# Opening of a four-layer graph network on one core: zero-padded node vectors, another order of fetches and sums

## The reference

```python
# block 0, _L0_gnn_ref (both supports are adj)
def _conv(x, adj):
    return x * jnp.sum(adj, axis=1)[None, :, None]
adaptive = jax.nn.softmax(jax.nn.relu(node_vec1 @ node_vec2), axis=1)   # 512x10 @ 10x512
outputs = [x]
for adj in (support0, support1, adaptive):
    x1 = _conv(x, adj)
    outputs.append(x1)
    for _ in range(2, ORDER + 1):
        x1 = _conv(x1, adj)
        outputs.append(x1)
out = jnp.concatenate(outputs, axis=2) @ W + b

# block 1, _L1_gnn_ref
A_norm = A + jnp.eye(n)
deg = jnp.sum(A_norm, axis=0) + jnp.sum(A_norm, axis=1) - jnp.diagonal(A_norm)
dinv = jax.lax.rsqrt(deg)
A_hat = A_norm * dinv[:, None] * dinv[None, :]
agg = jnp.einsum('nm,bmd->bnd', A_hat, features)
# then two linear layers with batch norms, relu between them
```

## Time and profile before

| | |
|---|---|
| Median of 3 runs | 937.22 us (935.61 to 937.93) |
| Profiled execution | 935.11 us |
| Its span in the profile | 933.3 us |
| TensorE (PE) busy | 893.1 us, 96% |
| VectorE (DVE) busy | 671.3 us, 72% |
| ScalarE (ACT) busy | 564.8 us, 61% |
| GpSimd (POOL) busy | 327.6 us, 35% |
| Instructions | 14540 |

### The profile page before, as it was taken

One profiled execution on the slowest core, in us unless ns is written; L12 is line 12 of the kernel. 1 busy time (PEld: TensorE's weight loads), 2 busy tenths in 40 slices (PEclk: granted clock), 3 DMA queues, 4 the chain that ended last, 5 costly groups with the idle time before them and its releaser, 6 DMA issues.

```text
span 933.3 us, 14540 instructions
## 1 busy us (share of the span) xinstructions
PE 893.1 (96%) x4990; PEld 774.3 (83%) x4990; DVE 671.3 (72%) x1589; ACT 564.8 (61%) x1230; POOL 327.6 (35%) x531
## 2 busy tenths in 40 slices
PE   9899999988989899999999999999999999999996
PEld 6788886366777689989989898998889898978986
DVE  6789996776687676677676767767776777675744
ACT  6477675944655565477457647765774775476341
POOL 3856554820122511362144216303521531340121
PEclk9999999999999899999999999999999999999999
DMA  5321201320110101001101200120110001001000
GB/s 186 136 68 62 74 36 46 135 87 6 34 58 1 34 1 57 2 23 35 57 1 46 69 1 12 35 69 1 46 39 31 12 12 46 1 12 34 1 23 24
DMA packets 26595, 38.55 MB, mean 41 GB/s; under 512 B 3333, under 2 KB 12422, under 8 KB 26010
## 3 DMA queue, kind: packets, MB, share of 16 engines
q1 hardware_dynamic: 26088, 36.05, 11.5%
q10 hardware_dynamic: 434, 1.57, 0.5%
HBM read 21.89 MB, written 15.73 MB: 40 GB/s over the span
## 4 chain that ended last, share of the span: by engine, by line
PE 50%; DVE 10%; ACT 8%; POOL 7%; issue 3%; ACTq 0%; DVEq 0%; POOLq 0%
PE psum L141 14%; PE psum L143 14%; PE psum L142 14%; PE psum L1867 2%; PE psum L1863 2%; PE psum L1864 2%; ACT gate L1438 2%; POOL out_rstd L1371 1%; ACT raw L1469 1%; POOL node_l L1389 1%; POOL x_rstd L1371 1%; ACT x L1469 1%; ACT raw L1532 1%; DVE cell L1584 1%; ACT gate L1441 1%
## 5 line engine op out<-in xcount | busy, mean ns | idle before, releaser
L1438 ACT ACTIVATE gate<-psum,gate_bias 128x256 f32<-128x256 f32 (+2 forms) x296 | 143.8, 557 | 67.7 <-PE psum L1867 54.4
L141 PE MATMUL psum<-in_h,wih_h 128*128 128x256 f32 (+2 forms) x312 | 106.8, 342 | 8.7 <-DVE in_l L1605 5.0
L143 PE MATMUL psum<-in_h,wih_l 128*128 128x256 f32 (+2 forms) x312 | 103.5, 332 | 0.0
L142 PE MATMUL psum<-in_l,wih_h 128*128 128x256 f32 (+2 forms) x312 | 103.1, 330 | 0.0
L141 PEld LDWEIGHTS psum<-in_h,wih_h 128*128 128x128 f32 x312 | 59.0, 189 | 21.2 <-DVE in_l L1605 8.6
L1405 POOL TENSOR_TENSOR gate<-in_h,in_l 128x512 f32<-128x512 f32 x14 | 17.9, 1306 | 157.5 <-DVE in_l L1605 157.5
L1441 ACT ACTIVATE gate<-cell 128x512 f32<-128x512 f32 (+2 forms) x80 | 40.3, 503 | 49.5 <-DVE cell L1589 39.1
L1586 DVE TENSOR_TENSOR gate<-gate 128x256 f32<-128x256 f32 (+2 forms) x48 | 24.1, 502 | 58.8 <-ACT gate L1438 58.7
L141 PE MATMUL psum<-e_h,shared 128*128 128x384 f32 x180 | 62.0, 344 | 2.2 <-POOL e_l L1420 2.0
L142 PEld LDWEIGHTS psum<-in_l,wih_h 128*128 128x128 f32 x312 | 59.2, 190 | 5.1 <-issue 0.2
L143 PEld LDWEIGHTS psum<-in_h,wih_l 128*128 128x128 f32 x312 | 58.9, 189 | 4.7
(11 more groups left out here) (394 smaller groups left out, 2894.2 us busy)
## 6 DMA issues: line engine op xcount, KB each, us to landing
x_spill<-x SPq DMA_DIRECT2D x30, 256.0 KB, 2.0
xt<-in_x_t_dram SPq DMA_DIRECT2D x16, 256.0 KB, 2.6
raw<-x_spill SPq DMA_DIRECT2D x16, 256.0 KB, 2.8
o_spill<-xt SPq DMA_DIRECT2D x14, 256.0 KB, 2.0
xt<-o_spill SPq DMA_DIRECT2D x14, 256.0 KB, 3.4
x<-x_spill SPq DMA_DIRECT2D x14, 256.0 KB, 3.6
out_dram<-raw SPq DMA_DIRECT2D x14, 256.0 KB, 2.3
raw<-in_adj_t_dram ACTq DMA_DIRECT2D x1, 1024.0 KB, 8.8
```

The costliest lines, as they stand in the source:

```text
L141: pe.matmul(dst, lh, rh, start=start, stop=False, **kw)
L142: pe.matmul(dst, lh, rl, start=False, stop=False, **kw)
L143: return pe.matmul(dst, ll, rh, start=False, stop=stop, **kw)
L1438: nc.scalar.activation(gate[q][:, 0:n], banks[GATE_BANK[q]][:, 0:n], ACT.Tanh if q == 2 else ACT.Sigmoid, bias=gate_bias[:, p - 1, q:q + 1 ...
```

## The change

- `nv1s` and `nv2s` become all 128 partitions of their regions. VectorE fills both with zeros behind `ones`; SP waits for that (`cleared`, 2) before it issues anything. The vectors still land in the first 10 partitions, and the logits matmuls contract over 128.
- Eight matmuls on `ones` instead of four.
- The transposed adjacency is issued on SP's queue, behind `adjn`, instead of on ScalarE's.
- The sums of three row tiles on VectorE come before the maximum of logits tile 3. ScalarE copies the bias rows before exp of tile 1. Exp of tile 3 goes between the scales of tiles 0 and 1, the last row tile's sum behind scale of tile 1, followed by all four column sums.
- Scale of tile 0 waits for the three row sums alone, that of tile 3 for the last one.
- In slot 0, combine of tiles 0 and 1 is cut in two: blocks 2 and 0 of both tiles, then the softmax factors, then blocks 3 and 4 of both, then the last row's copy and square, then `ask_dinv`. Tiles 2 and 3, and all later slots, are combined whole, with block 0 last as before.

```diff
@@ -178,7 +178,7 @@
         mix = sb("mix", [P, 2, 2, NT, D])
         aggh, aggl = sb("aggh", [P, 2, N], F32R), sb("aggl", [P, 2, N], F32R)
         z = sb("z", [P, HT, B, N])
-        nv1s, nv2s = z[0:RANK, 0, 0, :], z[0:RANK, 0, 1, :]
+        nv1s, nv2s = z[:, 0, 0, :], z[:, 0, 1, :]
         diag, squares = (z[:, 1, i, :].rearrange("p (t d) -> p t d", d=P) for i in range(2))
         spread_out = z[:, 0, 8:13, :].rearrange("p b n -> p (b n)")
         ahat = spread_out[:, 0:NT * N].rearrange("p (t n) -> p t n", n=N)
@@ -264,11 +264,13 @@
 
         @block.sync
         def _(sp):
-            sp.dma_start(nv1s, nv1_t).then_inc(c_nv, 16)
-            sp.dma_start(nv2s, nv2).then_inc(c_nv, 16)
+            sp.wait_ge(cleared, 2)
+            sp.dma_start(nv1s[0:RANK, :], nv1_t).then_inc(c_nv, 16)
+            sp.dma_start(nv2s[0:RANK, :], nv2).then_inc(c_nv, 16)
             for i in range(2):
                 sp.dma_start(xt[:, i, :], x_t[i]).then_inc(xt_loaded[i], 16)
             sp.dma_start(adjn[:], adj_n).then_inc(c_adjn, 16)
+            sp.dma_start(adjt, adj_t).then_inc(c_adjt, 16)
             for dst, src in ((w1raw, w1_t), (w2[:], w2_t), (bn1s[:], bn1), (bn2s[:], bn2), (wgs[:], wg), (bihs[:], bih), (bhhs[:], bhh)):
                 sp.dma_start(dst, src).then_inc(c_rest, 16)
 
@@ -436,7 +438,6 @@
             act.dma_start(ident[:], eye).then_inc(c_w, 16)
             act.dma_start(wraw[:], l0_w).then_inc(c_w, 16)
             act.dma_start(bias0[:], l0_b).then_inc(c_w, 16)
-            act.dma_start(adjt, adj_t).then_inc(c_adjt, 16)
 
             def split_x(q, i):
                 act.wait_ge(xt_loaded[i], 16 * (q + 1))
@@ -469,20 +470,23 @@
             relu_logits(1)
             relu_logits(2)
             exp_logits(0)
-            exp_logits(1)
             relu_logits(3)
-            exp_logits(2)
-            act.wait_ge(c_adjn, 16)
-            nc.scalar.activation(adjn[:, NT - 1, :], adjn[:, NT - 1, :], ACT.Identity, accum_out=coef[:, 0, NT - 1:NT]).then_inc(row_summed, 1)
-            exp_logits(3)
-            act.wait_ge(bias_spread, 1)
+            act.wait_ge(pe_setup, NT + 1)
             for i in range(2):
                 ins = nc.scalar.copy(bias_rows[:, i, :], tile(banks[3][:], 0))
             ins.then_inc(bias_ready, 1)
+            exp_logits(1)
+            exp_logits(2)
+
+            def sum_last_row():
+                act.wait_ge(c_adjn, 16)
+                nc.scalar.activation(adjn[:, NT - 1, :], adjn[:, NT - 1, :], ACT.Identity, accum_out=coef[:, 0, NT - 1:NT]).then_inc(row_summed, 1)
 
             def scale_first(q, t):
                 act.wait_ge(prod_done, NT * q + t + 1)
                 if q == 0 and t == 0:
+                    act.wait_ge(rows_summed, 1)
+                if q == 0 and t == NT - 1:
                     act.wait_ge(row_summed, 2)
                 nc.scalar.activation(mix[:, q % 2, :, t, :], scaled_block(t, 1), ACT.Identity,
                                      scale=coef[:, 0, t:t + 1]).then_inc(scaled, 1)
@@ -540,13 +544,14 @@
                 if now:
                     scale_first(q, 0)
                 if q == 0:
-                    sum_columns((0, 1))
+                    exp_logits(3)
                 if one and q > 1:
                     norm(q - 1, 0, range(NT))
                 if now:
                     scale_first(q, 1)
                 if q == 0:
-                    sum_columns((2, 3))
+                    sum_last_row()
+                    sum_columns(range(NT))
                 if q == 1:
                     norm(0, 0, range(NT))
                     split_ahat()
@@ -622,7 +627,8 @@
         def _(dve):
             chain = Chain(dve, dve1)
             roots = Roots(asked, rooted, exponent)
-            nc.vector.memset(ones[:], 1.0).then_inc(ones_ready, 1)
+            nc.vector.memset(ones[:], 1.0).then_inc(cleared, 1)
+            nc.vector.memset(z[:, 0, 0:2, :], 0.0).then_inc(cleared, 1)
 
             dve.wait_ge(c_w, 48)
             nc.vector.tensor_tensor(wmix[:, 0, :], wraw[:, 0, :], ident[:], ALU.add)
@@ -639,16 +645,22 @@
             nc.vector.tensor_tensor(wmix_l[:], wmix, f32(wmix_h[:]), ALU.subtract).then_inc(weights_ready, 1)
             logits_max(1)
             logits_max(2)
+            dve.wait_ge(c_adjn, 16)
+            nc.vector.reduce_sum(coef[:, 0, 0:NT - 1], adjn[:, 0:NT - 1, :], AX_X).then_inc(rows_summed, 1)
             logits_max(3)
-            dve.wait_ge(c_adjn, 16)
-            chain.link(nc.vector.reduce_sum(coef[:, 0, 0:NT - 1], adjn[:, 0:NT - 1, :], AX_X))
-            dve.wait_ge(row_summed, 1)
-            nc.vector.tensor_copy(row_sums[:], coef[:, 0, :]).then_inc(row_summed, 1)
-            nc.vector.tensor_tensor(coef[:, 1, :], coef[:, 0, :], coef[:, 0, :], ALU.mult)
-            dve.wait_ge(exp_ready, NT)
-            chain.link(nc.vector.reciprocal(smax[:, 3, :], smax[:, 2, :]))
-            chain.link(nc.vector.tensor_tensor(coef[:, 2, :], smax[:, 2, :], smax[:, 3, :], ALU.mult))
-            chain.link(nc.vector.tensor_tensor(coef[:, 3, :], coef[:, 2, :], coef[:, 2, :], ALU.mult))
+            dve.wait_ge(rows_summed, 1)
+            chain.link(nc.vector.tensor_tensor(coef[:, 1, 0:NT - 1], coef[:, 0, 0:NT - 1], coef[:, 0, 0:NT - 1], ALU.mult))
+
+            def softmax_sums():
+                dve.wait_ge(exp_ready, NT)
+                chain.link(nc.vector.reciprocal(smax[:, 3, :], smax[:, 2, :]))
+                chain.link(nc.vector.tensor_tensor(coef[:, 2, :], smax[:, 2, :], smax[:, 3, :], ALU.mult))
+                chain.link(nc.vector.tensor_tensor(coef[:, 3, :], coef[:, 2, :], coef[:, 2, :], ALU.mult))
+
+            def last_row():
+                dve.wait_ge(row_summed, 1)
+                nc.vector.tensor_copy(row_sums[:], coef[:, 0, :]).then_inc(row_summed, 1)
+                chain.link(nc.vector.tensor_tensor(coef[:, 1, NT - 1:NT], coef[:, 0, NT - 1:NT], coef[:, 0, NT - 1:NT], ALU.mult))
 
             def ask_dinv():
 
@@ -662,7 +674,7 @@
             def scale_ahat():
 
                 dve.wait_ge(dinv_spread, 1)
-                dve.wait_ge(pe_setup, NT + 1)
+                dve.wait_ge(pe_setup, NT + 2)
                 for t in range(NT):
                     ins = nc.vector.scalar_tensor_tensor(out=ahat[:, t, :], in0=adjt[:, t, :], scalar=dinv[:, t:t + 1],
                                                          in1=banks[7][:], op0=ALU.mult, op1=ALU.mult)
@@ -674,14 +686,20 @@
                 dve.wait_ge(dinv_squared, 1)
                 nc.vector.tensor_tensor(on_diagonal, on_diagonal, squares, ALU.add).then_inc(ahat_ready, 1)
 
-            def combine(q, t):
+            def combine(q, t, blocks=(2, 3, 4, 0)):
 
                 m = mix[:, q % 2, :, t, :]
                 dve.wait_ge(scaled, NT * q + t + 1)
-                for k in (2, 3, 4):
-                    chain.link(nc.vector.scalar_tensor_tensor(out=m, in0=scaled_block(t, k), scalar=coef[:, k - 1, t:t + 1],
-                                                              in1=m, op0=ALU.mult, op1=ALU.add))
-                nc.vector.tensor_tensor(m, m, scaled_block(t, 0), ALU.add).then_inc(mixed, 1)
+                for k in blocks:
+                    if k == 0:
+                        ins = nc.vector.tensor_tensor(m, m, scaled_block(t, 0), ALU.add)
+                    else:
+                        ins = nc.vector.scalar_tensor_tensor(out=m, in0=scaled_block(t, k), scalar=coef[:, k - 1, t:t + 1],
+                                                             in1=m, op0=ALU.mult, op1=ALU.add)
+                    if k == blocks[-1] and blocks != (2, 0):
+                        ins.then_inc(mixed, 1)
+                    else:
+                        chain.link(ins)
 
             def count_z(q, i):
                 b = 2 * q + i
@@ -733,11 +751,17 @@
                 nc.vector.tensor_tensor(low, whole, f32(high), ALU.subtract).then_inc(kept_lo, 1)
 
             def slot(q, now, more, one, two):
-                if now:
+                if q == 0:
+                    for t in range(2):
+                        combine(q, t, (2, 0))
+                    softmax_sums()
+                    for t in range(2):
+                        combine(q, t, (3, 4))
+                    last_row()
+                    ask_dinv()
+                elif now:
                     combine(q, 0)
                     combine(q, 1)
-                if q == 0:
-                    ask_dinv()
                 if q == PAIRED:
                     norm_last()
                     for i in range(2):
@@ -825,14 +849,14 @@
                 for _ in range(times):
                     pe.matmul(banks[bank][:], wmix_h[:, 0, :], operand[:, 0:N], start=True, stop=True)
 
-            pe.wait_ge(ones_ready, 1)
-            for _ in range(4):
+            pe.wait_ge(cleared, 1)
+            for _ in range(8):
                 pe.matmul(tile(banks[0][:], 0), ones[:], ones[:], start=True, stop=True)
```

(4 more changed lines are left out.)

4 lines of the change are left out of this document (2 added, 2 removed).

## The result

The changed kernel takes 938.99 us (median of 14 runs, 937.52 to 940.66) against 935.86 for the kernel before (14 runs, 935.01 to 938.6): a ratio of 1.0031, 95% interval 1.0023 to 1.0040, or 2.9 us slower. The range held it, by 2 us at its upper end; the case that the prediction thought likeliest, +0.7 us and no measurable difference, is not what happened. The ratio is just past the 0.3% that was given 0.12, and its interval lies on both sides of it.

A forecast was written before the change was run, and what follows sets the result against it. TensorE is busy 96% of the span, but VectorE carries the opening; 1.2 us gained before the first combine, 0.8, 0.6, 0.3 and 0.2 spent behind it, net +0.7: 937.22 becomes 937.9. Range 935.4 to 940.7, each widened by 0.3 noise.

The forecast's parts named there:

- the case that the prediction thought likeliest: Opening: gains given back in the split mix, without a fall of the clock; +0.7 us, 937.9 us, 45%.
- the 0.3% that was given 0.12: Whole kernel: chance 0.12 of being slower by over 0.3% (2.8 us).
- Zero fill and its wait on SP: Before the logits: fill 0.9 us, node vectors land at 4.5; warming matmuls start logits at 4.9, 1.7 us later.
- Zero rows: 128-row logits matmuls: zeros cost nothing; clock rises somewhere in the first two, if 128 rows count for it.
- S: Time in us of the first relu, on tile 0's logits: taken as 6.7, spanning 6.1 to 7.0.
- Three engines up to the first combine: VectorE, ScalarE, TensorE in the opening arrive within 0.3 us; first combine at 13.8 instead of 14.98, 1.2 us gained.
- The halved mix: Slot 0, tiles 0 and 1: 0.8 us waiting for tile 1, 0.6 softmax, 0.3 last row, 0.2 links spent.
- The stop behind it: TensorE idles 3.25 us before tile 2's products; a clock fall would cost tile 2 up to 0.6 us, tile 3 1.2.
- Adjacency: Copy by rows lands about 9.8 instead of 11.4 us; the transposed one near 12.7, its delay costing nothing.
- The case with this mechanism: Rival: TensorE's stop before tile 2 drops the clock; +0.7 plus 0.6 to 1.5 us, 939.0 as the middle, 22%.

The follow-up runs named there:

- with ten rows: The changed kernel with 10-row logits, no zero fill, no SP wait and four warming matmuls: 940.38 us, 1.0049 against the kernel before.
- the staged halves: The staged kernel with the mix of tiles 0 and 1 in halves again, nothing else: 938.19 us, 1.0016 against the kernel before.
- `W` behind: The changed kernel with the fetch of `W` on ScalarE's queue held back until the node vectors have landed: 946.68 us, 1.0100 against the kernel before.
- the filled stop: The changed kernel with 14 unused matmuls into a free bank in TensorE's slot 0 stop behind tile 1's products: 937.73 us, 1.0019 against the kernel before.
- the two runs with the zero rows: The kernel before with zero fill, SP's wait, 128-row logits, eight warming matmuls: 940.75 us; the same with the transposed adjacency behind the other on SP's queue: 936.43 us.
- the run with the zero rows alone: The kernel before with only the zero fill, SP's wait, 128-row logits and eight warming matmuls: 940.75 us, 1.0048.
- the staged kernel: The changed kernel, node vectors fetched aside and copied over cleared rows, no SP wait, mix whole, exp of tile 3 early, six warming matmuls, four later: 935.25 us.
- the order alone: The changed kernel with 10-row logits, no fill or SP wait, four warming matmuls, mix whole, exp of tile 3 before the first scale: 936.43 us, 0.9996.
- the mix whole again: The changed kernel with tiles 0 and 1 combined whole, after the softmax factors: 937.63 us, 1.0015 against the kernel before.

## Why the prediction was partly right

The range held, the likeliest case did not, and that 937.9 lies within 1.1 us of the measured 938.99 is luck: it was counted from 937.22, the median of three runs, where 14 give 935.86. The change itself was forecast at +0.7 us and measured at 2.9 to 3.1. At combine of tile 2 the forecast had +0.7 and the trace has +3.3. The 2.6 us between them are 1.5 at the first combine (15.32 instead of 13.8), 1.4 waiting for tile 2's products where none was forecast, and -0.3 in the halves. By its own steps:

- **Zero fill and its wait on SP**: the fill of 0.9 us was right (0.91). The landing at 4.5 was wrong: it reused the 2.0 us from issue to landing of the earlier trace rows for a transfer that the same wait had moved behind `W`. It landed at 5.83 in the changed kernel, at 8.0 with the transposed adjacency ahead too, and by 4.24 with neither. This is the step that failed first. The text looked at what SP's wait delays, and not at what overtakes it on the other queue.
- **Zero rows**: that they cost nothing was right (at the low level a record starts every 0.85 us with 128 rows, 7.70 to 8.56, as with ten), and that the clock rises in them too; the moment was not. The forecast had it in the first two logits matmuls (S = 6.7); in the changed kernel the clock rose in the third and S was 7.94. In other executions the eight records took 3.70 us from the first one on (5.61), so this term has a spread of a microsecond and more. By the rule of the Trainium skill (TensorE: Matmul & The Clock Gate, Part 1: The HAM clock gate), that the level follows how busy the engine has recently been, ten rows and 128 should have behaved alike. The trace disagrees: ten-row logits stayed at loads of 330 ns for 7.19 us, and those of 128 rows reached 190 ns at 10.18.
- **Three engines up to the first combine**: S plus 7.0, 6.3 and 4.6 was right in structure. From the real S, 7.94, they give 14.9 for the first combine, 14.2 for the first scale and 12.5 for the first product; measured were 15.32, 14.73 and 12.69. The forecast gain of 1.2 us turned into a loss of 0.34: 1.24 us through S (0.93 the late start, 0.31 the low level in the first matmul), and the other 0.3 behind it.
- **The halved mix**: the wait for tile 1 was forecast at 0.8 and measured 0.80. From the first combine to the end of ask-dinv were 6.9 us in the forecast and are 6.6, so that this part costs 1.6 us more than before where 1.9 was forecast.
- **The stop behind it**: forecast 3.25 us, measured 3.25. That the clock might fall was named, at 22%, and priced at 0.6 for tile 2; it fell in the changed kernel, with ten rows, in the staged halves and with `W` behind, in every unfilled case of this stop, and cost 1.0 us at combine 2 (the filled stop). Chance and size were both too low: the row of 33.66 had shown this sequence, a stop of 3.1 us and the clock at 0.50 behind it. And the stop cost 0.4 us even with the clock kept (the wait of 0.38 in the filled run), where the forecast had tile 2's scale just in time.
- **Adjacency**: by rows it landed at 11.1 (3.79 and 7.3) and not at 9.8, still ahead of the row sums at 12.29, so this was without cost; and placing the transposed one behind it is worth some 5 us to a kernel whose SP waits (1.0048 and 0.9994, the two runs with the zero rows), which the forecast did not have.
- The case with this mechanism stood at 939.0 us, which is the measured time by luck: the first combine came 1.5 us later than it had, and the base of 937.22 was 1.4 above the median of the 14 runs.

What stays open: why the landing of the node vectors varies from 5.2 to 5.8 us with the same order of issues, and what sets the moment of the clock's rise; both were seen and not varied. Rows and warming were not separated either: every run with ten rows had four warming matmuls, every one with 128 rows six or eight. Against warming as the cause speaks the run with the zero rows alone, where TensorE stood still for 3.18 us between the two and the clock rose 5.3 us into the 128-row logits.

## What to carry to other kernels

A wait put in front of a queue's first issue lets everything on the other queues overtake it: for the small transfer that opens the program, price what will stand ahead of it, not its own bytes; fetching it at once to another place and copying it over (0.68 us on VectorE) was part of the two versions that were clearly faster than before. Splitting work so that its first half can start earlier also finishes the first whole unit later; follow who waits for the whole one, here TensorE, whose stop of over 3 us made VectorE wait 0.4 us even at the kept clock and 1.4 with the fallen one. Where such a stop can't be avoided, filling it with matmuls into a free bank kept the clock at 1.00 in all three kernels and paid about 1 us in each, by ratios that are each at the edge of what they can tell; the staged kernel with the stop of slot 1 filled, at 932.96 us, beats both kernels.

## What the hardware showed that I had not expected

- 40 KB of node vectors landed 1.7 us after their second issue with only 64 KB issued ahead, 2.7 to 3.3 us with another 448 KB on the other queue, and 5.5 us with 1.5 MB; `W` (448 KB), issued at 4.24 behind 1.5 MB and beside 1 MB, had landed at 12.94.
- Plain f32 matmuls of 10 rows kept TensorE busy for 7.19 us without a rise of the clock, in all four profiles that have them (weight loads of 330 ns), and over the same ones with 128 rows, 118 of them zeros, it rose within the eight records in all nine, which also had more warming matmuls ahead of them.
- Of 15 stops of TensorE of 3.06 to 3.49 us in slots 0 and 1, 13 went with a fall of the clock; the two without (the order alone and the mix whole again, 3.06 us in slot 1) were as long as four others with one. The fall came between 1 us before the work resumed (ten rows: the granted clock is 0.83 from 18.5 to 19.0 us and 0.50 behind it, the work resumed at 19.80) and 1.5 us after (`W` behind: about 27.7 after 26.26). One stop of 1.78 us was followed by a fall too (the mix whole again, clock 0.62 from 12 to 13 us).
